# Where the layer norms' scales are computed, where a bias is added, and where two tiles are turned, in a six-stage transformer kernel

## The reference

```python
def _layernorm(x, axis=-1, eps=1e-05):
    m = jnp.mean(x, axis=axis, keepdims=True)
    v = jnp.var(x, axis=axis, keepdims=True)
    return (x - m) / jnp.sqrt(v + eps)
...
x = x + _L0_xattn_ref(_layernorm(x), ctx_512, ctx_512, ...)   # 16 heads, 1601 keys
x = x + _L0_attn_ref(_layernorm(x), ...)                      # state space, 16 heads of 32
x = x + _L0_ffn_ref(_layernorm(x), ...)                       # routed, 4 of 16 blocks
x = x + _L1_xattn_ref(_layernorm(x), ctx_512, ctx_512, ...)   # one head, 1601 keys
x = x + _L1_attn_ref(_layernorm(x), ...)                      # one head of 64
x = x + _L1_ffn_ref(_layernorm(x), ...)                       # fake-quantized, 1536 hidden
```

## Time and profile before

| | us |
|---|---|
| three executions, median | 1680.76 |
| lowest and highest of them | 1679.1 and 1686.83 |
| the profiled execution | 1682.18 |
| its span (first to last instruction) | 1680.5 |
| TensorE busy | 1549.7 (92%) |
| VectorE busy | 1195.5 (71%) |
| ScalarE busy | 878.2 (52%) |
| GpSimd busy | 723.9 (43%) |

### The profile page before, as it was taken

How to read it: one execution, slowest core, us unless ns; L and a number is a source line. 1 busy time by engine, 2 the same in 40 slices (tenths; PEclk the granted TensorE clock), 3 DMA queues, 4 the chain that set the end, 5 groups by cost and what they waited for, 6 DMA issues and landing times. The chain is left out here.

```text
span 1680.5 us, 33759 instructions
## 1 busy us (share of the span) xinstructions
PE 1549.7 (92%) x13881; PEld 811.9 (48%) x13990; DVE 1195.5 (71%) x2049; ACT 878.2 (52%) x1176; POOL 723.9 (43%) x348
## 2 busy tenths in 40 slices
PE   6999999999999999999878889999889989899469
PEld 3445555555555555555453545344535544444134
DVE  6688888888888888888566558998832244527981
ACT  1387777777777777777544213431112221327650
POOL 1467888888887888876404832330000000000000
PEclk9999999999999999999989989999999999899779
DMA  3489999999999999999923644669699942000001
GB/s 139 126 181 194 186 195 191 189 199 185 196 189 199 190 194 188 188 201 166 195 87 107 222 167 150 158 165 213 177 421 416 377 181 127 1 0 1 0 1 51
DMA packets 554667, 282.02 MB, mean 168 GB/s; under 512 B 481664, under 2 KB 532608, under 8 KB 551440
## 3 DMA queue, kind: packets, MB, share of 16 engines
q1 hardware_dynamic: 554512, 279.84, 70.4%
HBM read 138.74 MB, written 22.54 MB: 96 GB/s over the span
## 5 line engine op out<-in xcount | busy, mean ns | idle before, releaser
L604 POOL TENSOR_TENSOR x<-x_prob,x 128x1604 bf16<-128x1604 f32 x120 | 387.9, 3232 | 144.0 <-ACT x L769 144.0
L899 DVE TENSOR_REDUCE x_negmax<-x_score 128x1 f32<-128x1604 f32 x128 | 233.7, 1826 | 17.5 <-PE x_score L645 7.3
L759 ACT ACTIVATE x_prob<-x_score,x_negmax 128x1604 f32<-128x1604 f32 x128 | 204.8, 1600 | 25.7 <-DVE x_negmax L899 21.0
L628 PE MATMUL x_ring<-x_ctx_hi,wk_split 128*128 128x400 bf16 (+1 forms) x1024 | 216.2, 333 | 0.3 <-DVE x_kT L827 0.3
L628 PE MATMUL x_ring<-wv_split,x_ctx_hi 128*128 128x512 bf16 (+1 forms) x770 | 200.3, 379 | 9.7 <-issue 6.9
L827 DVE SCALAR_TENSOR_TENSOR x_kT<-x_ring,bk,x_kT 128x400 bf16<-128x400 f32 (+1 forms) x256 | 162.3, 635 | 31.7 <-ACT x_kT L748 23.9
L769 ACT CAST x<-x_prob 128x1604 bf16<-128x1604 f32 x120 | 183.0, 1525 | 0.0
L833 DVE TENSOR_TENSOR x_v<-x_ring,x_v 128x512 bf16<-128x512 f32 (+1 forms) x208 | 143.8, 691 | 52.8 <-ACT x_v L752 50.0
L748 ACT ACTIVATE x_kT<-x_ring,bk 128x400 bf16<-128x400 f32 (+1 forms) x196 | 116.5, 594 | 90.7 <-PE x_ring L628 89.8
L752 ACT CAST x_v<-x_ring 128x512 bf16<-128x512 f32 (+1 forms) x148 | 86.7, 586 | 97.0 <-PE x_ring L628 97.0
L628 PEld LDWEIGHTS x_ring<-x_ctx_hi,wk_split 128*128 128x128 bf16 x1024 | 93.8, 97 | 87.0 <-issue 19.4
(11 more groups left out here) (305 smaller groups left out, 2398.1 us busy)
## 6 DMA issues: line engine op xcount, KB each, us to landing
y_ctx<-in_ctx SPq DMA_DIRECT2D x16, 1664.0 KB, 12.3
y_ctxT<-in_ctxT SPq DMA_DIRECT2D x16, 1601.0 KB, 19.5
x_stage<-in_ctxT SPq DMA_DIRECT2D x48, 400.0 KB, 4.6
x_q_rows<-q_rows SPq DMA_DIRECT2D x64, 128.0 KB, 3.1
m_xT<-in_L_ffn_w SPq DMA_DIRECT2D x16, 512.0 KB, 4.6
ffn_w_parts<-m_xT SPq DMA_DIRECT2D x32, 256.0 KB, 2.7
x_stage<-in_ctxT SPq DMA_DIRECT2D x16, 401.0 KB, 4.7
f_w<-ffn_w_parts SPq DMA_DIRECT2D x4, 1024.0 KB, 8.4
```

Of the source, the lines that this page charges most:

```text
L604: pool.tensor_tensor(ph[:, g % 2, 1, 0:NKP], prob[:, g % 2, :], ph[:, g % 2, 0, 0:NKP], ALU.subtract).then_inc(pl_done, 1)
L628: last = pe.matmul(out_, lhs, rhs, start=(i == 0), stop=(i == len(steps) - 1))
L759: nc.scalar.activation(prob[:, g % 2, :].rearrange("p (c n) -> p c n", n=QW), scores, ACT.Exp, bias=nmax[:, g % 2:g % 2 + 1], accum_out=rs ...
L899: dve.tensor_reduce(nmax[:, pair % 2:pair % 2 + 1], scores, mybir.AxisListType.XY, ALU.max, negate=True).then_inc(max_done, 1)
```

## The change

Three things differ.

1. **The scales.** `norm_scales` and its calls are gone. `tile_stats` stays at each residual add. Every block now begins with `small_on_vector` for all eight tiles: eight aggregates, one operation, the root on ScalarE (with a load of the root's table before it), a reciprocal, four small operations, and in the shared forms the shift. Only then are tiles normalized. Since ScalarE uses the root's table in between, loads of the exponential's table come in ahead of the routing softmax and of the self attention's softmax.
2. **The bias in the state space.** The eight adds of b_out move from units 4 to 11 to behind the eight gate copies.
3. **The queries.** TensorE first runs 15 identity products, then turns tiles 0 to 5, makes the first half's two groups, turns tiles 6 and 7, and makes the second half.

```diff
-    def tile_stats(self, dve, x, t, done, counted):
+    def tile_stats(self, dve, x, t, done):
 
         dve.wait_ge(*done)
-        dve.bn_stats(self.stats[:, t, :], x[:, t, :]).then_inc(counted, 1)
-
-    def norm_scales(self, dve, first, last, step, base):
...
+        dve.bn_stats(self.stats[:, t, :], x[:, t, :])
...
     def on_vector(self, dve):
+        self.small_on_vector(dve)
+        self.hat_on_vector(dve, range(NT))
+
+    def small_on_vector(self, dve):
+        before = NT if self.loaded else 0
         if self.loaded:
-            self.small_on_vector(dve)
-            self.hat_on_vector(dve, range(NT))
-        else:
-            self.hat_on_vector(dve, range(NT // 2))
-            self.last_scales_on_vector(dve)
-            self.hat_on_vector(dve, range(NT // 2, NT))
...
     def on_scalar(self, nc, act):
+        self.root_on_scalar(nc, act)
+        act.wait_ge(self.s_shift, 1)
         for t in range(self.HALF, NT):
-            if t == NT - 1:
-                act.wait_ge(self.s_var, self.LAST_SCALES)
...
     def on_vector(self, dve):
+        self.small_on_vector(dve)
+        dve.scalar_tensor_tensor(self.shift[:], self.meanvar[:, :, 0], -1.0, self.rstd[:, :, 0], ALU.mult,
+                                 ALU.mult).then_inc(self.s_shift, 1)
         self.hat_on_vector(dve, range(self.HALF))
-        self.last_scales_on_vector(dve)
...
                                   bG[:, n // 2:n // 2 + 1], None, ALU.add).then_inc(s_gT, 1)
+                dve.tensor_tensor(x[:, n, :], x[:, n, :], bO[:], ALU.add).then_inc(s_xo, 1)
...
-                if 4 <= n < 4 + NT:
-                    dve.tensor_tensor(x[:, n - 4, :], x[:, n - 4, :], bO[:], ALU.add).then_inc(s_xo, 1)
...
-                if t == NT - 1:
-                    k.norm_scales(dve, 0, NT - 1, s_stats, NT - 1)
...
-            norm.on_tensor(pe)
+            k.keep_busy(pe, ident, banks[3], 15)
+            for t in range(NT - 2):
+                norm.turn_on_tensor(pe, t)
             for n, (m, c) in enumerate(kgroups):
+                if (m, c) == (0, 1):
+                    norm.turn_on_tensor(pe, NT - 2)
+                    norm.turn_on_tensor(pe, NT - 1)
```

More of the change, by code:

```diff
@@ L55, in __init__ @@
         self.used = []
-        self.stats = self.meanvar = self.rstd = self.shift = None
+        self.stats = None
         self.x = None
@@ L75, in sem @@
         return self.used[-1]
-    def tile_stats(self, dve, x, t, done, counted):
+    def tile_stats(self, dve, x, t, done):
         dve.wait_ge(*done)
-        dve.bn_stats(self.stats[:, t, :], x[:, t, :]).then_inc(counted, 1)
-    def norm_scales(self, dve, first, last, step, base):
-        ve, r, u = self.meanvar[:, first:last, 1], self.rstd[:, first:last, 0], self.shift[:, first:last]
-        if base:
-            dve.wait_ge(step, base)
-        for t in range(first, last):
-            dve.bn_aggr(self.meanvar[:, t, :], self.stats[:, t, :]).then_inc(step, 1)
-        done = base + last - first
-        dve.wait_ge(step, done)
-        dve.tensor_scalar(ve, ve, EPS, None, ALU.add).then_inc(step, 1)
-        dve.wait_ge(step, done + 1)
-        dve.tensor_scalar(r.bitcast(I32), ve.bitcast(I32), 1, None, ALU.logical_shift_right).then_inc(step, 1)
-        dve.wait_ge(step, done + 2)
-        dve.tensor_scalar(r.bitcast(I32), r.bitcast(I32), -1.0, ROOT_SEED, ALU.mult, ALU.add).then_inc(step, 1)
-        done += 3
-        for _ in range(3):
-            dve.wait_ge(step, done)
-            dve.scalar_tensor_tensor(u, r, -0.5, r, ALU.mult, ALU.mult).then_inc(step, 1)
-            dve.wait_ge(step, done + 1)
-            dve.tensor_tensor(u, u, ve, ALU.mult).then_inc(step, 1)
-            dve.wait_ge(step, done + 2)
-            dve.scalar_tensor_tensor(r, u, 1.5, r, ALU.add, ALU.mult).then_inc(step, 1)
-            done += 3
-        dve.wait_ge(step, done)
-        dve.scalar_tensor_tensor(u, self.meanvar[:, first:last, 0], -1.0, r, ALU.mult, ALU.mult).then_inc(step, 1)
+        dve.bn_stats(self.stats[:, t, :], x[:, t, :])
     def keep_busy(self, pe, ident, bank, count):
@@ L129, in __init__ @@
         self.loaded = loaded
-        self.k = k
         if home is None:
-            self.meanvar, self.rstd = k.meanvar, k.rstd
+            self.stats = k.sb(ctx, name + "_stats", [P, NT, 6]) if loaded else k.stats
+            self.meanvar = k.sb(ctx, name + "_meanvar", [P, NT, 2])
+            self.rstd = k.sb(ctx, name + "_rstd", [P, NT, 1])
+            self.small = k.sb(ctx, name + "_small", [P, 4, NT])
         else:
@@ L210, in root_on_scalar @@
     def root_on_scalar(self, nc, act):
-        if not self.loaded:
-            return
         act.wait_ge(self.s_var, 1)
@@ L241, in __init__ @@
         super().__init__(k, ctx, name, x, ident, banks, xT)
-        self.shift = k.shift
+        self.shift = k.sb(ctx, name + "_shift", [P, NT])
+        self.s_shift = k.sem(ctx, name + "_shift_done")
         self.s_hat_act = k.sem(ctx, name + "_xhat_scalar_done")
@@ L2322, in _ @@
         def _(act):
+            act.wait_ge(norm.s_var, 1)
+            nc.scalar.activation(norm.small[:, 1, :], norm.small[:, 0, :], ACT.Sqrt).then_inc(norm.s_root, 1)
+            act.wait_ge(s_shift, 1)
             for t in range(NT // 2, NT):
-                if t == NT - 1:
-                    act.wait_ge(norm.s_var, norm.LAST_SCALES)
-                nc.scalar.activation(xhat[:, t, :], x[:, t, :], ACT.Identity, bias=k.shift[:, t:t + 1],
+                nc.scalar.activation(xhat[:, t, :], x[:, t, :], ACT.Identity, bias=shift[:, t:t + 1],
                                      scale=norm.rstd[:, t, :]).then_inc(s_hat2, 1)
```

51 lines of the change are left out of this document (16 added, 35 removed).

## The result

| | before | after |
|---|---|---|
| median of four executions, us | 1681.38 | 1668.91 |
| lowest and highest | 1679.1 and 1686.83 | 1668.36 and 1670.2 |
| profiled execution, span | 1680.5 | 1667.4 |
| TensorE busy | 92% | 94% |

The ratio of after to before is 0.9929, with a 95% interval of 0.9912 to 0.9947: 0.7% faster, 9 to 15 us. The forecast was 1669.7 us. So the total was right; whether the sum was right is a matter of its terms. In what follows T0 is the start of VectorE (DVE) in a new block, as in the prediction.

The account below looks back on a forecast made before the run. TensorE is busy for most of the span, so hand-overs, state-space loop and queries were judged separately: -2.6 - 0.6 - 5.56 - 1.05 + 1.8 + 0 - 3.05 = -11.05 us from 1680.76, giving 1669.7; 8-in-10 range 1665.5 to 1676.5.

Parts of the forecast that it names:

- First hand-over, -2.6: Cross attention 0 to state space: without the scales block ahead of the last residual add, T0 comes 2.6 us earlier.
- Clock in the state-space stage, -0.6: State-space start: the rise to full clock comes up to 2.6 us earlier, saving 0 to 1.3; middle taken, -0.6 us.
- Bias, -5.56: State-space units 4 to 14: removing adds slowed by GpSimd saves 5.56 us; beside the gate copies they cost 0.
- State space to feed-forward, -1.05: Hand-over to block feed-forward: last add 1.15 us earlier, first tiles behind T0 0.1 later, -1.05 us in sum.
- self attention to last feed-forward, -3.05: Hand-over to last feed-forward: the whole 3.1 us scales block was on the path, T0 + 4.59 against 4.56 behind; -3.05 us.
- Cross attention to self attention, 0: Hand-over to self attention: the block was just hidden and the value weights' load decides the start; 0 us.
- Queries, +1.8: Cross-attention queries: T0 stays, but TensorE waits for tile 7's copy, so the second half starts later; +1.8 us.
- Rival (a): All new block starts: ScalarE's table switch costs twice, 5.0 us in all, total 1674.7 us (1675.1 with drain); chance 0.12.
- (b): Hand-overs: bound by something other than VectorE, so only the bias is won, total 1676.5 us; chance 0.08.
- (d): State-space loop: the bias move wins only half, GpSimd slowing units for another reason, total 1672.5 us; chance 0.06.
- (e): Cross-attention queries: TensorE stays at 1.2 GHz, slower than before, total 1687 us; chance 0.05.
- Rival (c): Queries: the last two tiles cost +0.9 instead of +1.8, by earlier start or quicker copy, 1668.8 us; chance 0.12.

Follow-up runs that it names:

- bias_alone: Kernel before with only the eight bias additions moved from units 4 to 11 to behind the gate copies; ratio to before 0.9970.
- order_only: Changed kernel without the 15 identity products in the queries, new order kept; one execution, first score product at T0 + 28.70 us.
- ident_only: Changed kernel with all eight query tiles turned ahead of the products, the 15 identity products kept; ratio to before 0.9927.
- scales_alone: Changed kernel with the bias and queries edits undone, so only the new scales differ from the kernel before; ratio to before 0.9964.
- queries_old: Changed kernel with the queries as before: all eight tiles turned ahead of the products, no identity products; ratio to before 0.9919.
- busy_starts: ident_only plus 22 and 12 identity products around the first two turned tiles of state space and block feed-forward; ratio to before 0.9898, median 1664.74 us.
- root_ready: busy_all plus one activation of the root's function at the end of ScalarE's program in five stages; ratio to before 0.9892.
- busy_all: busy_starts with more identity products in the last feed-forward (26 for 15, 30 for 18); ratio to before 0.9877.
- router_first: busy_all with a separate semaphore for the router's weights and 8 instead of 12 identity products before that wait, in block feed-forward; ratio to before 0.9875.
- longer_fill: root_ready with 22 instead of 12 identity products before the feed-forward's small-load wait, 20 instead of 12 in state space; ratio to before 0.9911.

## Why the prediction was right, point by point

**First hand-over, -2.6.** Right: stretch 2 lost 2.47 in the pair; two kernels of the old kind show 10.27 and 9.94, the four of the new one in the table 7.58 to 7.81.

**Clock in the state-space stage, -0.6.** The pair shows -0.55 in stretch 3, which looks like a hit and is none. With the old hand-over the stretch is 42.32 and 41.55 (bias_alone), with the new one, without fillers, 40.95 to 42.39. What it follows is how long behind the stage's first product the granted clock rises: 4.4 us before, 2.8 in bias_alone, 3.3 in the changed kernel, 1.6 in order_only (40.95) and 4.6 in ident_only (42.39). In all nine traces without fillers there, a later rise goes with a longer stretch, 0.5 us for each us, and the new hand-over does not make the rise earlier (2.8 and 4.4 us with the old one, 1.6 to 4.6 with the new). The step that failed is that a shorter gap ahead of the products brings this rise forward. Its worth is not to be told from zero; only the fillers took the low clock away (40.18 in all five kernels that have them).

**Bias, -5.56.** Right to the last digit, and so is the cause that I gave: GpSimd beside DVE, and not the transfers.

**State space to feed-forward, -1.05, and self attention to last feed-forward, -3.05.** Right: stretch 4 gives -6.69 for bias and this hand-over, so -1.13 ahead of T0, where I had 1.15; behind T0 the third tile is turned at T0 + 5.52 for T0 + 5.31, 0.2 later where I had 0.1. Stretch 9 gives -3.40, 0.35 more than forecast, half of it ahead of T0: from the last product's end to T0 5.52 before and 2.24 after, so -3.28 where I had 3.1 for the block alone. The other half is behind T0, -0.12 where I had +0.05.

**Cross attention to self attention, 0.** Right: stretch 8 differs by 0.08.

**Queries, +1.8.** The number was right (T0 + 27.41 for T0 + 25.53, +1.88), its reason was half wrong. I wrote that for DVE's next work the two orders of the scales are equal, that the identity products go unnoticed, and that what is lost is the order alone. In fact there are three terms: the new scales make PE wait 3.2 us behind T0, so that its turned tiles come later and meet the slow clock (+2.0 to +2.3, scales_alone and queries_old); the identity products take 2.1 of that back; the new order costs 1.7. The step that failed is the one that looked only at DVE's stream. A reader who undid the reordering because of my text would have gained 1.7; one who undid the whole edit would have lost 0.4 (27.84 for 27.41). That these terms add up to nearly the forecast +1.8 is luck.

**What ends the feed-forward.** I took T0 of the queries to stay where it was against DVE's last addition. In all fourteen traces it follows the end of SyncE's last issue of a weight store (the row at 1194.72) by 3.81 to 3.90 us, and the landing of that store by 1.91 to 2.00, while its distance from the last addition varies from 3.0 to 7.0. In the program SyncE's last act in the block is to wait for that landing. So the store is what the barrier waits for, which is why 0.3 us of the forecast went here and 1.5 of busy_starts' gain.

**The rest.** Stretches 5, 7 and 10 add +0.54 in the pair and stretch 1 takes 2.59; by the other columns both are chance. Without stretch 1 the pair differs by 10.5 us, with a forecast of 11.05. Added up, my terms give -11.06, not -11.05, and the chances of forecast and rivals 1.01; neither matters here. Rival (a) is refuted, (b) and (d) by the stretches, (e) by the first two groups of the queries, 7.11 us at full clock (granted 1.00). Rival (c), 1668.8, is nearer the median than the forecast, but its mechanism is not there.

## What to carry to other kernels

Work that is moved behind a barrier is paid twice if TensorE waits for it: once as time, and once in the clock of what TensorE does next. Products of no use in that gap are worth it, but only if no second gap follows. A wait for several loads, of which only the first is needed, can be such a gap; a semaphore of its own for the first should remove it, though no trace here caught the loads late with that semaphore in place. And an elementwise step with both inputs in SBUF belongs where GpSimd rests.

## What the hardware showed that I had not expected

- The granted clock stayed at 0.50 for 10 to 14 us of nearly unbroken work in the start of the block feed-forward (turned tiles, router products and the first hidden ones; 13.5 us in the changed kernel, 10.3 in root_ready). With 22 and 8 (or 12) identity products around the first two tiles it stayed at 1.00 over the same work where PE did not idle again (busy_starts, busy_all, router_first), and fell where it idled 1.15 or 1.35 us behind them (root_ready, longer_fill).
- The last of the five small loads, issued at T0 + 2.0 to 2.2, landed between T0 + 5.3 and T0 + 7.2 from one trace to the next, and at T0 + 7.7 in longer_fill, where it was issued at T0 + 3.3. Between busy_starts (last addition at T0 + 204.0) and longer_fill (T0 + 213.0) 4.7 of the 9.0 us are there already at the first hidden product, T0 + 10.7 and T0 + 15.4.
- Whether the first products of the last feed-forward meet the full clock differs between kernels whose code is the same there (before and bias_alone, scales_alone and ident_only): stretch 10 is 225.2 to 226.6 where they do, and 227.5 to 227.9 where they do not (bias_alone, queries_old, ident_only). No kernel has two traces, so that it changes between executions of one kernel is likely and not shown.
